# First attention of a four-block image network: copies of values on GpSimd, filler matmuls, and the tail of the attention by halves of the images

## What is computed

```
def _ln_t(v, eps=1e-05):
    m = jnp.mean(v, axis=-1, keepdims=True)
    s = jnp.var(v, axis=-1, keepdims=True)
    return (v - m) / jnp.sqrt(s + eps)

def _L0_conv_ref(x, Wq, bq, Wk, bk, Wv, bv):
    q = jnp.einsum('oc,bchw->bohw', Wq, x) + bq[:, None, None]
    k = jnp.einsum('oc,bchw->bohw', Wk, x) + bk[:, None, None]
    v = jnp.einsum('oc,bchw->bohw', Wv, x) + bv[:, None, None]
    k_unf = _unfold(k)
    v_unf = _unfold(v)          # 7 x 7 neighbourhood, zero padding
    attn = jnp.einsum('bchw,bcphw->bphw', q, k_unf)
    attn = jax.nn.softmax(attn, axis=1)
    return jnp.einsum('bphw,bcphw->bchw', attn, v_unf)
...
    x = x + _L0_conv_ref(_ln_c(x), L0_conv_Wq, ..., L0_conv_bv)
    t = _to_tokens(x)
    t = t + _L0_ffn_ref(_ln_t(t), L0_ffn_router_w, ...)
```

## Time and profile before

| what | value |
|---|---|
| median of three runs | 417.6 us (416.93 to 417.88) |
| the profiled execution | 417.61 us, its span in the trace 415.7 us |
| mean granted clock of TensorE in it | 0.988 of full speed |
| busy: PE, DVE, ACT, POOL | 379.2, 331.9, 289.8, 165.5 us |
| first attention, from its first scores to the first row of `norm(1)`'s result | 11.5 to 31.3 us |

### The profile page before, as it was taken

One profiled execution on the slowest core, in us unless ns is written; L12 is line 12 of the kernel. 1 busy time (PEld: TensorE's weight loads), 2 busy tenths in 40 slices (PEclk: granted clock), 3 DMA queues, 4 the chain that ended last, 5 costly groups with the idle time before them and its releaser, 6 DMA issues.

```text
span 415.7 us, 9843 instructions
## 1 busy us (share of the span) xinstructions
PE 379.2 (91%) x3994; PEld 260.5 (63%) x3994; DVE 331.9 (80%) x656; ACT 289.8 (70%) x516; POOL 165.5 (40%) x140
## 2 busy tenths in 40 slices
PE   6789999989899898899999998989999999999897
PEld 5576942223236766676777665667678787666575
DVE  3859797998974478899999588999997686999451
ACT  4846296998946479997770599987822627999471
POOL 5002200000000049889998278999994050000000
PEclk9988999999999999999999999999999989999999
DMA  8300040000007000000000000000000000000000
GB/s 297 143 2 0 2 97 2 2 0 2 2 0 278 0 2 2 2 3 2 1 2 2 2 2 2 2 2 2 2 2 1 2 2 1 2 2 1 2 2 27
DMA packets 1629, 9.29 MB, mean 22 GB/s; under 512 B 208, under 2 KB 976, under 8 KB 1104
## 3 DMA queue, kind: packets, MB, share of 16 engines
q1 hardware_dynamic: 1440, 8.59, 5.8%
q10 hardware_dynamic: 144, 0.07, 0.1%
HBM read 7.40 MB, written 0.26 MB: 18 GB/s over the span
## 4 chain that ended last, share of the span: by engine, by line
PE 34%; DVE 32%; ACT 16%; POOL 8%; issue 8%; DMA 1%; DVEq 0%; SPq 0%; ACTq 0%
PE bank L1398 6%; PE bank L1128 4%; DVE PRD L985 4%; DVE wb L985 4%; POOL PRD L374 3%; PE bank L1478 3%; ACT RINGS L599 3%; ACT RINGS L669 2%; DVE RINGS L883 2%; ACT RINGS L602 2%; DVE RINGS L874 2%; POOL wb L374 2%; PE bank L1387 2%; DVE SMT L997 2%; PE bank L1274 2%
## 5 line engine op out<-in xcount | busy, mean ns | idle before, releaser
L1478 PE MATMUL bank<-VB,RINGS 64*128 64x144 f32 x1152 | 93.0, 298 | 5.9 <-DVE PRD L985 3.0
L1478 PEld LDWEIGHTS bank<-VB,RINGS 64*128 64x128 f32 x1152 | 75.6, 186 | 27.7 <-issue 10.1
L1128 PE MATMUL bank<-cst 128*128 128x128 f32 x422 | 59.4, 284 | 0.0
L357 POOL TENSOR_TENSOR HY<-OM,cst 128x324 f32<-128x324 f32 x16 | 11.5, 748 | 116.8 <-DVE LXA L930 113.0
L1128 PEld LDWEIGHTS bank<-cst 128*128 128x128 f32 x422 | 53.1, 195 | 5.2 <-issue 2.8
L985 DVE TENSOR_TENSOR wb<-bank,HY 128x864 f32<-128x864 f32 x48 | 50.3, 1049 | 4.6 <-PE bank L1478 4.5
L985 DVE TENSOR_TENSOR PRD<-bank,HY 128x864 f32<-128x864 f32 x48 | 50.0, 1049 | 4.0 <-PE bank L1478 4.0
L599 ACT ACTIVATE RINGS<-bank,cst 128x768 f32<-128x768 f32 x48 | 42.4, 883 | 15.3 <-PE bank L1461 15.1
L602 ACT ACTIVATE RINGS<-RINGS,cst 128x768 f32<-128x768 f32 x48 | 44.9, 936 | 1.6
L540 ACT ACTIVATE RINGS<-PRD,wb 128x2048 f32<-128x2048 f32 (+1 forms) x21 | 39.5, 1921 | 4.5 <-PE bank L1398 3.4
L1398 PE MATMUL bank<-RINGS,cst 128*32 128x512 f32 x336 | 39.7, 594 | 2.4 <-DVE RINGS L883 2.0
(11 more groups left out here) (277 smaller groups left out, 704.0 us busy)
## 6 DMA issues: line engine op xcount, KB each, us to landing
wd<-in_wd SPq DMA_DIRECT2D x1, 2793.0 KB, 9.6
wb<-in_wb SPq DMA_DIRECT2D x1, 2112.0 KB, 10.2
wc<-in_wc SPq DMA_DIRECT2D x1, 1027.0 KB, 12.2
cst<-in_cst SPq DMA_DIRECT2D x1, 766.0 KB, 5.1
PRD<-PRD SPq DMA_DIRECT2D x1, 324.0 KB, 3.7
PRD<-PRD SPq DMA_DIRECT2D x1, 323.9 KB, 5.0
PRD<-PRD SPq DMA_DIRECT2D x1, 323.8 KB, 4.4
XC<-in_x SPq DMA_DIRECT2D x2, 128.0 KB, 2.4
```

The lines of the kernel that those rows point to most:

```text
L1128: pe.matmul(bk[:, 0:P], ident, ident, start=True, stop=True)
L1478: ins = pe.matmul(view(bank[q % 2 * 2 + gp], k3 * NR, [[3 * NR, 2 * CG], [1, NR]]), view(HX, b % 2 * HXN + (3 * t + k3) * NPIX + half * P, ...
```

## The change

The change keeps all arithmetic, and moves or splits this:

- The two copies into VZ go from ACT to GpSimd, as `tensor_copy`, at the end of its clearings and ahead of `top2(0)`.
- PE gets three fills ahead of `turn(4)` (`FILL_TURN`), two after the turns and two after `values(1)` (`FILL_VALUES`); `FILL[1]` goes from 18 to 12.
- PE transposes YG by halves (`yg_half`): half 0 behind `turn(7)` and ahead of `values(1)`, half 1 behind it. They use banks 4 and 5.
- DVE divides, adds XT, sums and centres half 0 and then half 1, in eight operations of 256 columns, each waiting for the one before. Then come the sums of squares and the scaling as before.
- ACT loads the Sqrt table after e0, ahead of the second copy into YG, and no longer at the start of `deviations(1)`.

```
+FILL_TURN, FILL_VALUES = 3, 2
-FILL, FILL_EC = (13, 18, 12, 6, 5, 9, 12, 8), 2
+FILL, FILL_EC = (13, 12, 12, 6, 5, 9, 12, 8), 2
+        yg_bank = (bank[4], bank[5])
...
+            def other_values():
+                pool.wait_ge(vz_clear, 1)
+                pool.wait_ge(lxa_clear, 1)
+                pool.wait_ge(vt_ready, 1)
+                for j in range(2):
+                    mine, other = (view(t, at * B4 * C, [[2 * B4 * C, 2], [1, B4 * C]], 64 * j, 64)
+                                   for t, at in ((VZ, j), (VT, 1 - j)))
+                    pool.tensor_copy(mine, other).then_inc(vz_ready, 1)
...
+            other_values()
             pool.wait_ge(pa_set, 2)
             top2(0)
...
             def deviations(n, eps):
-                table(ACT.Sqrt)
+                if n != 1:
+                    table(ACT.Sqrt)
...
                     if s == B4:
-                        act.wait_ge(vz_clear, 1)
-                        act.wait_ge(vt_ready, 1)
-                        for j in range(2):
-                            mine, other = ...
-                            act.activation(mine, other, ACT.Copy).then_inc(vz_ready, 1)
...
                         act.activation(e0[:, 0:NT], den[:, 0:NT], ACT.Exp).then_inc(pad_ready, 1)
+                        table(ACT.Sqrt)
                     act.wait_ge(av_done, bh + 1)
...
-            dve.wait_ge(yg_turned, 1)
-            link(dve.tensor_tensor(tiles(Y2), tiles(bank[4]), per_tile(den), ALU.mult))
-            dve.wait_ge(xt_kept, 1)
-            link(dve.tensor_tensor(XT[:, :], XT[:, :], Y2[:, :], ALU.add))
-            norm(1)
+            for bh in range(NBH):
...
+                dve.wait_ge(yg_turned, bh + 1)
+                link(dve.tensor_tensor(y, view(yg_bank[bh], 0, [[C, NT // 2], [1, C]]), per_half(den, bh), ALU.mult))
+                dve.wait_ge(xt_kept, 1)
+                link(dve.tensor_tensor(x, x, y, ALU.add))
+                link(dve.tensor_reduce(one(s16, bh), x, AX.X, ALU.add))
+                dve.scalar_tensor_tensor(xn, per_half(s16, bh), -1.0 / C, x, ALU.mult, ALU.add).then_inc(centred, 1)
...
+                def yg_half(bh):
+                    pe.wait_ge(yg_ready, bh + 1)
+                    for half in range(2):
+                        g = 2 * bh + half
+                        ins = pe.transpose(yg_bank[bh][:, half * P:(half + 1) * P], view(YG, g * P, [[1, P]]), ident)
+                    ins.then_inc(yg_turned, 1)
...
-                for s in range(1, B):
+                for s in range(1, B4):
                     turn(s)
-                    if s == 4:
-                        values(0)
+                keep_warm(bank[6], FILL_TURN)
+                turn(4)
+                values(0)
+                for s in range(5, B):
+                    turn(s)
+                yg_half(0)
+                keep_warm(bank[7], FILL_VALUES)
                 values(1)
+                keep_warm(bank[7], FILL_VALUES)
+                yg_half(1)
...
-            pe.wait_ge(yg_ready, 2)
-            for g in range(4):
-                ins = pe.transpose(bank[4][:, g * P:(g + 1) * P], view(YG, g * P, [[1, P]]), ident)
-            ins.then_inc(yg_turned, 1)
```

More of the change, by code:

```diff
@@ L466, in attend @@
                     if s == B4:
-                        act.wait_ge(vz_clear, 1)
-                        act.wait_ge(vt_ready, 1)
-                        for j in range(2):
-                            mine, other = (view(t, at * B4 * C, [[2 * B4 * C, 2], [1, B4 * C]], 64 * j, 64)
-                                           for t, at in ((VZ, j), (VT, 1 - j)))
-                            act.activation(mine, other, ACT.Copy).then_inc(vz_ready, 1)
                         act.wait_ge(pt_done, TURNED_BY_ACT + 1)
@@ L850, in _ @@
             link(dve.reciprocal(view(den, 0, [[8, 2], [4, 2], [1, 4]]), by_unit(e0)))
-            dve.wait_ge(yg_turned, 1)
-            link(dve.tensor_tensor(tiles(Y2), tiles(bank[4]), per_tile(den), ALU.mult))
-            dve.wait_ge(xt_kept, 1)
-            link(dve.tensor_tensor(XT[:, :], XT[:, :], Y2[:, :], ALU.add))
-            norm(1)
+            per_half = lambda t, bh: view(t, bh * NT // 2, [[1, NT // 2], [0, C]])
+            one = lambda t, bh: t[:, bh * NT // 2:(bh + 1) * NT // 2]
+            for bh in range(NBH):
+                at = bh * NPIX
+                x, y, xn = (view(t, at, [[C, NT // 2], [1, C]]) for t in (XT, Y2, XN))
+                dve.wait_ge(yg_turned, bh + 1)
[4 more added lines that the diff above has]
+                dve.scalar_tensor_tensor(xn, per_half(s16, bh), -1.0 / C, x, ALU.mult, ALU.add).then_inc(centred, 1)
+            for bh in range(NBH):
+                dve.wait_ge(sq_made, NBH + bh + 1)
+                dve.tensor_reduce(one(var, bh), view(SQ, bh * NPIX, [[C, NT // 2], [1, C]]), AX.X, ALU.add).then_inc(var_ready, 1)
+            for bh in range(NBH):
+                xn = view(XN, bh * NPIX, [[C, NT // 2], [1, C]])
+                dve.wait_ge(sd_ready, NBH + bh + 1)
+                link(dve.reciprocal(one(rstd, bh), one(sd, bh)))
+                dve.tensor_tensor(xn, xn, per_half(rstd, bh), ALU.mult).then_inc(xn_ready, 1)
+            dve.wait_ge(xn_ready, NBH * 2)
             dve.wait_ge(wb_s, 16)
```

## The result

| | median | lowest and highest |
|---|---|---|
| before | 417.5 us | 416.93 to 417.88 (4 runs) |
| after | 414.24 us | 413.79 to 414.83 (4 runs) |

The ratio is 0.9922, with a 95% interval of 0.9908 to 0.9936: 3.3 us less, against 2.9 forecast (414.7 us).

The account below looks back on a forecast made before the run. No engine bounds the whole; from 16 to 31 us one thread passes between engines. Terms 0.84 (ACT) + 1.01 (clock, turns) + 1.82 (DVE wait) - 0.73 (smaller operations) = 2.94 us, so 414.7 us; range 413.7 to 416.1.

Parts of the forecast that it names:

- e0: Work on ACT in the attention, not defined further in the text; forecast to end at 21.75, just before the table load.
- The copies leave ACT: Attention: without the VZ copies ACT starts its copy for step 2 at 17.14, not 17.98; 0.84 us less, turn(4) at 18.70.
- The clock: Attention, 20.2 to 23.5: fills and earlier values(0) keep the granted clock at 1.00, so values(0) takes 1.12 us, not 1.78.
- rival (a): Attention: the clock falls again at 20.2 for the same 3.3 us; gain 1.9 us, 415.7 us; chance 0.17.
- The turns and the last copy: Attention: DVE's copies run 20.88 to 22.59 at 0.57 each, against an end at 24.44 before; gain so far 1.85 us.
- rival (e): Attention: no effect, something other than ACT ends the waits, for instance DVE copies queued behind row maxima; chance 0.04 with other nulls.
- The table load: ACT, between e0 and the second YG copy: load 1.28 plus activation 0.20, done at 23.23 with 0.55 us of cover.
- Rival (b): ACT ahead of the second YG copy: the table load holds ACT 2.56 us, twice its row; 415.4 us; chance 0.06.
- The tail by halves: DVE after attention: half 0 starts without waiting for all of YG, 1.82 us gained, 0.73 lost to eight smaller operations.
- Rival (c): PE ahead of XN's transposes: fills at half clock end at 32.4, 1.0 us late; 418.6 us; chance 0.04.
- Rival (d): Experts' first matmuls, 33.8 to 37.1: the half-clock stretch moves or vanishes, up to 0.8 us more gain; 413.9 us; chance 0.10.
- clock and earlier turns: Attention up to the last copy: term of the sum for the kept clock and earlier turns, 1.01 us gained.

## Why the prediction held, step by step

*The copies leave ACT* (forecast 0.84): 1.01 up to `turn(4)`. The step was right, and of the other 0.17 us 0.14 is ACT's: its copy for step 2 held the engine 0.52 us before the next exponential and 0.38 now. Undone alone it costs 0.96 us in the trace and 1.3 to 1.5 in the time.

*GpSimd's price* (0.45 each, bounds 0.45 and 0.90): 0.85 for both. They ended at 18.43, and `values(0)` started at 20.11; no operation of DVE beside them is longer than before (0.41 and 0.55). That term was zero, as I had taken it.

*The clock.* This is the term that was right by its number and wrong in its reason. I had the fills keep the clock at 1.00; without them it stays there as well. And I took the fall of before as a property of that kernel: two kernels with the same idle 1.7 us kept the clock. So this idle stretch doesn't force the fall; rival (a) came in no trace with the copies on GpSimd. It has some weight in the medians all the same. A fall of 3.3 us takes 0.004 off the mean granted clock, so a run at 0.999 or 1.000 had none of that length. Among the 36 runs of before in the first two groups the twelve such runs took 416.4 to 417.2 us, the other 24 took 417.3 to 418.9. Of the changed kernel's four runs the one at 0.999 took 414.83 and the others 413.79 to 414.42. So where the clock didn't fall the difference is about 1.9 us (416.7, the twelve's median, less 414.83), near the 2.23 of the traces, and about 3.6 where it did (417.7 less 414.06). That a fall costs before more than the changed kernel fits the 1.13 us above; with four runs, and with starts that differ by 1 us as well, it is argued and not shown.

*The turns and the last copy* (22.59 - 13.24 = 9.35 forecast): 9.11. DVE copied three in 1.57 us and then waited for the last turn, that is for ACT's last exponential; so ACT and not DVE is late at that point, by 0.17 us. (The code has `turn(7)` wait for the last exponential and for the copy of step 4; that copy ended at 21.71, the exponential with its row sum at 22.27, and the turn started at 22.32.) On the way there a piece of rival (e) was real: DVE's copy of step 4 stands behind all the row maxima, which ended at 21.05, and began at 21.16, 6.81 us behind the first exponential where the sum's spacing (0.58 behind the start of its turn, 18.70) gives 6.04. It cost nothing, since three copies back to back were done by 22.73.

*Two transposes* ready within 0.82 us of the copy, and the fills of `yg_half` hidden: yes. *The table load* had 0.55 us of cover by forecast; it ended with its small activation at 24.15, 0.51 ahead of the YG copy. (The sum has e0 end at 21.75, where its rows give 21.65; nothing hung on that.) Rival (b) is out, and with it the whole worth of moving the load: nothing.

*The tail by halves* (1.82 less 0.73, 1.09): DVE's eight operations took 3.50 us for 2.87, so 0.63 and not 0.73, and the whole term is 1.27 by the trace of the undone version. Of that 0.12 us is in the sums of squares: half 0's is done early, and the rest of `norm(1)` went from 1.65 us (29.71 to 31.36) to 1.53.

*The 12 fills* ended 0.89 us ahead of XN's transposes (1.0 forecast). Rival (c) never came near, and the number didn't matter: 18 gave the same time (414.25).

*Rival (d)*, more by the routing: the fall at 33.8 is missing in the trace of after, as (d) has it, but only 0.1 us came of it (7.06 against 6.96 us from XN's transposes to the gates). My price of 0.8 us was wrong there, since it put all of PE's time on the path. DVE's operations fill most of that stretch (3.03 of 3.40 us in after).

*The reference.* The sum was held against one execution of before that had an early start (8.42) and a fall of the clock worth 1.13 us. These errors have opposite signs, and part of the closeness of 414.7 to 414.24 is theirs and so luck. The term "clock and earlier turns", forecast at 1.01, came to 1.08 in the table (2.09 less 1.01) only because that execution of before had its fall. Against before with 9 first fills, which had none, the last copy gains 0.96 (10.07 less 9.11), no more than `turn(4)` does, and the term is zero.

## What to carry to other kernels

Before a clock term is put into a sum, look whether the clock falls in the same place in several executions; in one trace it may be that run's. Work taken from an engine that stands between two others pays at once when a third has been idle and the result is wanted late: here the two copies on GpSimd alone brought 1.4 us. And fills ahead of a wait should be counted at their slowest rate: with 13 first fills the transposes started later than XN's second half was ready in nine of ten traces, by 0.2 to 1.5 us, and with 9 or 11 by 0.02 us at most in their four. Where several inputs arrive one after the other, ask which of them the next step needs last: six more fills ahead of `norm(1)` made the transposes start 0.29 us later, and it cost nothing.

## What the hardware showed that I had not expected

- At the start of the program TensorE ran 10 of these records in 1.8 us in one execution and 18 in the same 1.8 us in another, while the row of the granted clock said 1.00 throughout. The rate changed at about 6.6 us in one (before) and about 8.6 in the other (after). At the start the row doesn't tell the rate; the records do.
- 1.7 us without work for PE led to a clock of 0.50 in one execution and not in two others with the same instructions around it. What else decides it these runs can't tell. One rival to idle time stays untested: when the work falls. In the ten traces with 13 first fills the clock was low for longest where XN's first transposes started earliest, and not at all where they started last: 8.42 (three stretches at 0.50, from 20.2, 33.8 and 334 us), 8.59 (31 to 37.5), 8.79 (38 to 41.5), 9.24 (32 to 36 and 325 to 333), 9.29 (32 to 39), 9.45 and 9.53 (326 to 329.5), 9.54 (32.5 to 36.5), 9.88 and 9.96 (none before 412). But before with 9 first fills started at 7.96 and had none.
- A granted clock of 0.50 for 3 us or more cost 1.13 us in the attention, and between XN's transposes and the gates from nothing (copies on ACT without inner fills, 6.97 us against 6.96) to 0.7 (the same with fills, 7.69, where it lasted from 31 to 37.5): the price depends on where the fall lies.
